# Mixture of experts behind convolution and attention: fixed first tiles, a one-hot gather for slot 0, and a reordered convolution end and last slot

## The chip, the cores and the metric

The kernel runs on one core of a Trainium2 chip. The metric is the device time of one execution in microseconds (us); the version before has a median of 236.17 us over three runs (235.69 to 236.37).

## The reference

The input x has shape (8, 192, 16, 16): 8 images, 192 channels, 256 pixels. Three parts follow each other, all in float32:

```python
x = x + conv(group_norm(x))          # 1x1 convolution over 192 channels and 28 local correlations ("taps")
t = tokens(x)                        # (8, 256, 192)
t = t + attention(layer_norm(t))     # causal, one head, d = 192
n = layer_norm(t)
e = argmax(n @ Wg.T + bg)            # top-1 of 8 experts; its softmax over one value is 1
t = t + (silu(n @ W1[e].T) * (n @ W2[e].T)) @ W3[e].T     # inner width 469
```

## The kernel before, in words

All matrix products with rounded operands are made as sums of a high and a low part (names ending in H and L), so that each product of the reference is several matmuls. The kernel is written engine by engine in program order, with semaphores between the engines; nothing is reordered by a planner.

**Convolution.** A loop over i = 0 to 11 (LAG = 4) handles image i in its norm, and image i - 4 in its convolution. On TensorE, iteration i does near_gram (L1125), group_sums at i = 2 (L1063), near_norms (L1082), and from i = 4 on conv (L1103), turn_taps (L1093) and conv_taps (L1118). keep_busy (L1248) issues matmuls whose result nobody reads. On ScalarE copy_taps (L515) copies the transposed taps, take_u and norm_image(0) (L585, the input of attention for image 0) stand at i = 10, copy_taps behind them. In the same iterations VectorE computes statistics (token_stats, L757) and leftover(0) (L812), one quarter of the low parts of expert 0's weights; GpSimd computes token_factors (L396, whose last instruction is L408) and weights_lo (L410).

**Attention.** step(t), t = 1 to 9, on every engine: scores, softmax, values, residual of image t - 1, statistics of image t - 2. Beside it the weights of the experts are loaded into two stage buffers by SyncE (L292), split into high parts by ScalarE (L522) and low parts by GpSimd (L410) and VectorE (L812). Expert 6's and 7's low parts are made by VectorE alone, in six pieces each (low_weights, L787).

**Routing.** gate (L818) finds a token's expert; counts (L1193) and positions (L838) give each token its row in a table in HBM, `xs`: every expert has a region, and `run` holds the running count. The last images are gates 4 (image 6) and 5 (image 7), both in step 9. scatter_tokens (L438) writes a tile of 128 tokens with an indirect DMA on GpSimd's queue. Behind the last gate VectorE computes from `run` which of 23 slots belongs to which expert and where it starts (L981 to L1010, `slot_expert`, `slot_row`), then the six pieces of expert 6 (L1012). Slots are in the order of the experts.

**Slots.** SyncE waits for all scatters and the table, then loads slot j's 128 rows (load_slot, L338), at most two at a time. ffn_step(j) on TensorE (L1325), ScalarE (L643) and VectorE (L1026) has three parts: `back` (transpose of gh(j - 1), L1343; its high part HH, L646, and low part HL, L1029; the products with W3, L1367 and L1368), `mid` (ten matmuls, L1076 to L1080, silu L649, product L1034) and `nxt` (transpose of the normalised rows of slot j + 1, L1358, parts FH L652 and FL L1037). norm_slot (L1017) normalises a loaded slot. Two adds (L1047, L1049) give the output rows, which GpSimd sends with an indirect DMA (L478). In steps 0 to 5 VectorE also makes one piece of expert 7's low parts. fill(40) (L1321) stands on TensorE ahead of the slots.

The lines that the sums touch most:

```python
            SCATTERS = {4: (0,), 5: (1,), 6: (2,), 7: (3, 4), 8: (5,), 9: (6,)}
            scatter_tokens(IMAGES - 1)
            norm_slot(0, 0, 1)
            for j in range(-1, SLOTS + 1):
                ffn_step(j, j % 2, j > 0, 0 <= j < SLOTS, j < SLOTS - 1, j // 2 + 2 if j + 2 < SLOTS else None)
                if 0 <= j < 6:
                    low_weights(EXPERTS - 1, (j,))
```

## Time and profile before

| | |
|---|---|
| median of the runs (range) | 236.17 us (235.69 to 236.37) |
| profiled execution, its own time | 237.56 us |
| its span, first to last instruction | 235.7 us |
| busy: TensorE, VectorE, ScalarE, GpSimd | 212.4, 170.6, 113.9, 105.0 us |
| mean granted TensorE clock | 0.96 of full speed |
| first expert product, end of the last TensorE matmul | 136.64, 229.69 us |

The times in all rows are microseconds from the start of the span. PE is TensorE's matmuls, PEld its weight loads, DVE is VectorE, ACT ScalarE, POOL GpSimd, SP SyncE; L1076 is line 1076 of the kernel. In a timeline row stand start, length, engine, line, operation, what it writes and reads, how many were merged, and in brackets the idle time before it with what ended it.

### The profile page before, as it was taken

What the parts mean: (1) busy time and instruction counts of PE and PEld (TensorE: products, weight loads), DVE (VectorE), ACT (ScalarE), POOL (GpSimd) and SP (SyncE); (2) the same over time, 40 slices, a digit from 0 to 9 for tenths busy, and PEclk for the clock granted to TensorE, in tenths of its full rate; (3) what the DMA queues carried; (4) which work ended last, traced back from release to release, by engine and by line L of the source; (5) the groups of instructions that cost most, each with busy time, mean ns of one, the idle gap of its engine ahead of it and who ended that gap; (6) DMA issues with size and microseconds to landing.
All of it is one profiled execution on the core that took longest, in us unless ns stands there. A gap on an engine that the chain in (4) does not pass through costs nothing.

```text
span 235.7 us, 4722 instructions
## 1 busy us (share of the span) xinstructions
PE 212.4 (90%) x1336; PEld 187.4 (79%) x1336; DVE 170.6 (72%) x554; ACT 113.9 (48%) x244; POOL 105.0 (45%) x131
## 2 busy tenths in 40 slices
PE   6977999987999979998889979999999999999970
PEld 3667889976999968987667768999999999999960
DVE  3696897774379859699787857888686767686741
ACT  2475655363199978897540033333334343434310
POOL 3266663829009997996766001131313131313131
PEclk9996899997699999999999999999999999999995
DMA  6991277856600562656211122233210000010100
GB/s 240 392 341 49 72 185 192 208 158 248 233 0 0 201 229 84 241 218 228 110 54 53 51 56 73 79 88 79 69 38 2 33 8 21 17 36 2 35 12 0
DMA packets 16343, 26.13 MB, mean 111 GB/s; under 512 B 3863, under 2 KB 12755, under 8 KB 15424
## 3 DMA queue, kind: packets, MB, share of 16 engines
q1 hardware_dynamic: 14448, 22.66, 30.3%
q0 software_dynamic: 1872, 3.18, 4.0%
q8 instruction: 12, 0.20, 0.3%
q14 instruction: 11, 0.09, 0.1%
HBM read 19.76 MB, written 6.76 MB: 113 GB/s over the span
## 4 chain that ended last, share of the span: by engine, by line
PE 55%; DVE 17%; POOL 7%; issue 7%; ACT 6%; DMA 4%; POOLq 1%; SPq 0%; DVEq 0%; ACTq 0%
PE bank L1367 8%; PE bank L1343 4%; PE bank L1076 4%; PE bank L1078 4%; PE bank L1080 4%; PE bank L1079 4%; PE bank L1077 4%; PE bank L1368 4%; PE bank L1251 3%; DMA stage<-in_w_all 2%; PE bank L1122 2%; PE bank L1358 2%; POOL ln L405 1%; DVE rows L881 1%; POOL wall L418 1%
## 5 line engine op out<-in xcount | busy, mean ns | idle before, releaser
L478 POOL DMA_INDIRECT out_rows<-yo,rows x23 | 22.4, 972 | 79.9 <-DVE yo L1049 70.0
L1367 PE MATMUL bank<-wall,HH 128*128 x92 | 29.4, 375 | 1.5 <-DVE HL L1029 1.5
L1034 DVE TENSOR_TENSOR gh<-gh,bank 128x470 f32<-128x470 f32 x23 | 14.8, 645 | 18.8 <-PE bank L1080 18.8
L646 ACT ACTIVATE HH<-bank 128x512 fp32r<-128x512 f32 x23 | 13.8, 599 | 27.9 <-PE bank L1343 27.9
L1208 PE MATMUL bank<-mH 128*128 128x512 f32 x98 | 24.4, 394 | 0.0
L652 ACT ACTIVATE FH<-bank 128x256 fp32r<-128x256 f32 x23 | 8.8, 385 | 30.7 <-PE bank L1358 30.7
L1368 PE MATMUL bank<-wall,HL 128*128 x92 | 23.1, 252 | 0.0
L1076 PE MATMUL bank<-wall,FH 128*128 x46 | 19.3, 419 | 1.2 <-DVE FL L1037 1.2
L1208 PEld LDWEIGHTS bank<-mH 128*128 128x128 f32 x98 | 17.8, 188 | 3.2
L444 POOL DMA_INDIRECT token_rows<-rows,posi x16 | 17.0, 1065 | 6.7 <-issue 4.4
L649 ACT ACTIVATE gh<-bank 128x470 f32<-128x470 f32 x23 | 13.0, 564 | 12.5 <-PE bank L1080 12.5
L1367 PEld LDWEIGHTS bank<-wall,HH 128*128 128x128 f32 x92 | 17.3, 188 | 1.8 <-issue 1.7
L1029 DVE TENSOR_TENSOR HL<-bank,HH 128x512 fp32r<-128x512 f32 x23 | 15.9, 691 | 3.3 <-ACT HH L646 3.1
L1368 PEld LDWEIGHTS bank<-wall,HL 128*128 128x128 f32 x92 | 17.6, 192 | 0.0
L1080 PE MATMUL bank<-wall,FL 128*128 x46 | 17.3, 376 | 0.0
L1078 PE MATMUL bank<-wall,FL 128*128 x46 | 17.3, 376 | 0.0
L1079 PE MATMUL bank<-wall,FH 128*128 x46 | 17.3, 375 | 0.0
L1077 PE MATMUL bank<-wall,FH 128*128 x46 | 17.2, 374 | 0.0
L1343 PE MATMUL bank<-small_sb,gh 128*128 128x128 f32 x92 | 13.9, 273 | 0.7 <-DVE gh L1034 0.6
L415 POOL TENSOR_TENSOR wall<-stage,wall 128x940 fp32r<-128x940 f32 x6 | 13.5, 2258 | 1.5 <-ACT wall L529 1.5
L418 POOL TENSOR_TENSOR wall<-stage,wall 128x768 fp32r<-128x768 f32 x6 | 12.8, 2134 | 0.0
L495 ACT ACTIVATE f32t<-xcm,gnb,grs 128x256 f32<-128x256 f32 x16 | 8.7, 593 | 7.6 <-POOL gnb L373 7.6
(228 smaller groups left out, 645.1 us busy)
## 6 DMA issues: line engine op xcount, KB each, us to landing
stage<-in_w_all SPq DMA_DIRECT2D x7, 1324.0 KB, 5.7
rows<-token_rows SPq DMA_DIRECT2D x23, 98.0 KB, 2.0
near_rows<-gram SPq DMA_DIRECT2D x8, 243.0 KB, 3.1
xcm<-in_x_cm SPq DMA_DIRECT2D x2, 768.0 KB, 7.0
rows<-in_x_tm SPq DMA_DIRECT2D x1, 1536.0 KB, 12.7
stage<-in_w_all SPq DMA_DIRECT2D x4, 331.0 KB, 4.0
token_rows<-emptyt SPq DMA_DIRECT2D x3, 294.0 KB, 4.6
taps_sb<-near_rows SPq DMA_DIRECT2D x8, 103.0 KB, 2.1
```

Of the source, the lines that this page charges most:

```text
L444: pool.indirect_dma_start(out=xs, out_offset=bass.IndirectOffsetOnAxis(ap=posi[:, j:j + 1].bitcast(U32), axis=0), in_=rows[:, j], in_offse ...
L478: pool.indirect_dma_start(out=out, out_offset=bass.IndirectOffsetOnAxis(ap=rows[:, j, C + 2:C + 3].bitcast(U32), axis=0), in_=yo[:, par], ...
L1029: nc.vector.tensor_tensor(HL[:, 1 - par].rearrange("p k x -> p (k x)"), bank[5][:], HH[:, 1 - par].rearrange("p k x -> p (k x)").bitcast(F ...
L1076: nc.tensor.matmul(dst, xh_a, y_a, start=True, stop=False)
L1077: nc.tensor.matmul(dst, xh_a, yl_a, start=False, stop=False)
L1078: nc.tensor.matmul(dst, xl_a, y_a, start=False, stop=False)
L1079: nc.tensor.matmul(dst, xh_b, y_q, start=False, stop=False)
L1080: return nc.tensor.matmul(dst, xl_b, y_q, start=False, stop=not more)
L1208: nc.tensor.matmul(bank[6][:], mH[:, 0:P], mH[:], start=True, stop=True)
L1343: mm = nc.tensor.transpose(bank[5][:, P * k:P * (k + 1)], gh[:, 1 - par, P * k:P * (k + 1)], ident)
L1367: nc.tensor.matmul(dst[:, 0:2 * C], HH[:, 1 - par, k], w(0, P, c0, c0 + 2 * C), start=(k == 0), stop=False)
L1368: mm = nc.tensor.matmul(dst[:, 0:C], HL[:, 1 - par, k], w(0, P, c0, c0 + C), start=False, stop=(k == FT - 1))
```

## The change

1. Front, TensorE: keep_busy(2) twice at i = 2, ahead of group_sums(2) and behind near_norms(0).
2. End of the convolution: ScalarE's copy_taps(6) goes ahead of norm_image(0); VectorE waits for ln1_ready ahead of leftover(0); GpSimd waits for leftover(0) ahead of weights_lo(0).
3. The first eight slots are the first tiles of the eight experts, at fixed rows of `xs` and with fixed weights on TensorE. The table is only for the other 15 slots. Slot 0 is loaded as soon as images 0 to 5 are scattered. The tokens of images 6 and 7 that belong to slot 0 are not scattered (their row gets NOWHERE added); VectorE builds one-hot tables (find_first), TensorE multiplies the rows of these images by them (gather), and VectorE adds the product to slot 0's rows (complete_first).
4. fill(40) goes; fill(2), fill(5) and, in step 0, fill(8) come. norm_slot(1) moves behind slot 0's `mid`. The table's arithmetic is cut into three functions, before and behind norm_slot(0) and behind step -1. Pieces of experts 6 and 7 are made in pairs in steps 0 to 5.
5. Last slot: the products on HH are made by themselves as soon as HH is there, all into 192 columns, then those on HL; one VectorE add instead of two.

```diff
+EMPTY = EXPERTS * REGION + PAD
+NO_TOKEN = 4096
+MORE = SLOTS - EXPERTS
+LATE = IMAGES - 2
+NOWHERE = 1 << 20
-WARM = 40
...
+        in_first = [a[:, 0:2 * P].rearrange("p (h q) -> p h q", h=HALVES) for a in (sc_sb, Pr)]
+        first_row = bank[3][:, 0:ROW]
...
-            sp.wait_ge(scattered, 16 * TILES)
+            def load_first_tile(e):
+
+                at = REGION * e + PAD
+                sp.dma_start(rows[:, e], xs[at:at + P]).then_inc(slot_in[e % 2], 16)
...
+            sp.wait_ge(scattered, 16 * HALVES * LATE)
             sp.wait_ge(empty_out, 16 * HEAD_PARTS)
+            load_first_tile(0)
+            sp.wait_ge(gathered, 1)
+            sp.wait_ge(scattered_late, 16 * (TILES - HALVES * LATE))
+            for e in range(1, EXPERTS):
+                if e >= 2:
+                    sp.wait_ge(slot_in[e % 2], 16 * (e // 2))
+                load_first_tile(e)
             sp.wait_ge(table_ready, 1)
...
             token_factors(1)
+            pool.wait_ge(wall_q, 1)
             weights_lo(0)
...
                     take_u(0, 0)
+                if i >= LAG:
+                    copy_taps(i - LAG)
+                if i == IMAGES + 2:
                     sc.wait_ge(ln1_ready, 2)
                     norm_image(0)
-                if i >= LAG:
-                    copy_taps(i - LAG)
...
+                    link(nc.vector.tensor_scalar(rsum[:], at, float(PAD + P), float(NOWHERE), ALU.is_lt, ALU.mult))
+                    nc.vector.tensor_tensor(posi[:, HALVES * a:HALVES * z], at, rsum[:], ALU.add).then_inc(pos_ready, 1)
+
+            def find_first(b):
...
+                nc.vector.tensor_tensor(in_first[b - LATE], row, at, ALU.is_equal).then_inc(in_first_ready, 1)
...
-                    for g in (4, 5):
-                        gate(g, link)
-                        positions(g, link)
+                    gate(4, link)
+                    positions(4, link)
+                    gate(5, link)
+                    find_first(LATE)
+                    positions(5, link)
+                    find_first(LATE + 1)
...
                     low_u(0, 0)
+                    ve.wait_ge(ln1_ready, 2)
                     leftover(0)
...
+            def complete_first():
+
+                ve.wait_ge(gathered, 1)
+                ve.wait_ge(slot_in[0], 16)
+                nc.vector.tensor_tensor(rows[:, 0, 0:C + 2], rows[:, 0, 0:C + 2], first_row[:, 0:C + 2], ALU.add)
+                token = rows[:, 0, C + 2:C + 3].bitcast(I32)
+                nc.vector.tensor_tensor(token, token, first_row[:, C + 3:C + 4], ALU.add).then_inc(first_whole, 1)
+                ve.wait_ge(first_whole, 1)
...
+            table_tiles()
             nc.vector.memset(gh[:, :, FE:FT * P], 0.0)
-            low_weights(EXPERTS - 2, range(6))
...
+                    if j == SLOTS:
+                        nc.vector.tensor_tensor(yo[:, 1 - par], y[:, 0:C], row, ALU.add).then_inc(y_taken, 1)
+                        return
...
+            complete_first()
             norm_slot(0, 0, 1)
+            table_ends()
             for j in range(-1, SLOTS + 1):
-                ffn_step(j, j % 2, j > 0, 0 <= j < SLOTS, j < SLOTS - 1, j // 2 + 2 if j + 2 < SLOTS else None)
-                if 0 <= j < 6:
-                    low_weights(EXPERTS - 1, (j,))
+                if j == -1:
+                    ffn_step(j, 1, False, False, True)
+                    table_slots()
+                elif j == 0:
+                    ffn_step(j, 0, False, True, False)
+                    norm_slot(1, 1, 1)
+                    ffn_step(j, 0, False, False, True, 2)
+                else:
+                    ffn_step(j, j % 2, True, j < SLOTS, j < SLOTS - 1, j // 2 + 2 if j + 2 < SLOTS else None)
+                if 0 <= j < 3:
+                    low_weights(EXPERTS - 2, (2 * j, 2 * j + 1))
+                elif 3 <= j < 6:
+                    low_weights(EXPERTS - 1, (2 * j - 6, 2 * j - 5))
...
                     counts(5)
+                    gather(LATE)
+                    fill(2)
+                    gather(LATE + 1)
+                    fill(5)
+
+            def gather(b):
+
+                pe.wait_ge(in_first_ready, b - LATE + 1)
+                for h in range(HALVES):
+                    mm = nc.tensor.matmul(first_row, in_first[b - LATE][:, h], rows[:, HALVES * b + h, :], start=(b == LATE and h == 0), stop=(b == IMAGES - 1 and h == 1))
...
                 if i == 2:
+                    keep_busy(2, c1("gm"))
                     group_sums(2)
                 if 2 <= i < LAG:
                     near_norms(i - 2)
+                if i == 2:
+                    keep_busy(2, c1("gm"))
...
-            fill(WARM)
...
+                if j == 0:
+                    fill(8)
                 if nxt:
...
+                    if j == SLOTS:
+                        for k in range(FT):
+                            for s in range(2):
+                                c0 = 3 * W12 + C * (2 * k + s)
+                                nc.tensor.matmul(dst[:, 0:C], HH[:, 1 - par, k], w(0, P, c0, c0 + C), start=(k + s == 0), stop=False)
+                        pe.wait_ge(hl_ready, j + AHEAD)
```

## Rows read from the trace of the kernel before

**Rows 1.** Windows: busy us (and instructions) of each engine, granted clock, DMA share, GB/s.
```profile
core 0: us, PE busy (x) PEld busy (x) DVE busy (x) ACT busy (x) POOL busy (x), PEclk, DMA share, GB/s
16.40:20.35 3.95, 1.41 (x11) 1.23 (x11) 3.54 (x15) 1.42 (x5) 1.73 (x3) 0.83 0.34 120
18.99:25.81 6.82, 5.48 (x19) 4.28 (x18) 4.93 (x21) 5.49 (x12) 5.36 (x10) 0.50 0.23 72
...
56.54:63.37 6.83, 6.83 (x31) 6.67 (x31) 1.33 (x5) 1.40 (x5) 2.36 (x2) 0.50 0.69 259
...
134.90:138.30 3.40, 2.17 (x11) 1.70 (x11) 1.02 (x4) 0.68 (x2) 0.00 (x0) 1.00 0.25 65
140.00:225.00 85.00, 84.96 (x518) 78.21 (x518) 64.67 (x155) 33.66 (x65) 20.05 (x21) 1.00 0.15 42
```

**Rows 2.** Chain that ended last, in order of time: start, us, what.
```profile
26.08 0.11 PE bank L1137
...
78.14 5.42 DMA stage<-in_w_all
...
112.38 0.35 PE bank L1235 x2
```

**Rows 3.** Timeline of the front, TensorE and VectorE.
```profile
23.05 2.76 PE L1251 MATMUL bank<-small_sb 128*128 128x384 f32 x4
...
23.76 0.74 DVE L745 SCALAR_TENSOR_TENSOR gram<-bank,rn,rnb 128x192 f32<-128x192 f32 x2
```

**Rows 4.** Timeline of the convolution's end: TensorE, ScalarE, GpSimd.
```profile
53.93 0.39 PE L1100 MATMUL bank<-small_sb,taps_sb 128*104 128x128 f32 x2
...
56.47 1.61 PE L1122 MATMUL bank<-wtap,taps_t 104*128 104x192 f32 x4 [1.62 <-ACT taps_t L520]
...
55.16 0.98 ACT L593 ACTIVATE xn<-rows,ln 128x192 f32<-128x192 f32 x2 [2.09 <-POOL ln L408]
...
62.55 0.38 ACT L520 ACTIVATE taps_t<-bank 104x256 f32<-104x256 f32 x1 [5.43 <-PE bank L1100]
...
45.38 0.19 POOL L408 TENSOR_TENSOR ln<-ln 128x2 f32<-128x2 f32 x1
...
53.85 1.17 POOL L408 TENSOR_TENSOR ln<-ln 128x4 f32<-128x4 f32 x1
```

**Rows 5.** Chain that ended last, the transfers of the handover.
```profile
128.92 2.51 DMA token_rows<-rows,posi
...
132.41 1.95 DMA rows<-token_rows
```

**Rows 6.** Timeline of the handover from attention to the slots, all engines.
```profile
124.95 1.07 POOL L444 DMA_INDIRECT token_rows<-rows,posi  x1 [1.25 <-DVE posi L851]
...
126.66 0.16 DVE L851 CAST posi<-bank 128x2 int32<-128x2 f32 x1
...
128.84 0.34 DVE L1002 TENSOR_TENSOR started<-small_sb,ends 128x184 f32<-128x184 f32 x1
...
126.65 8.32 PE L1208 MATMUL bank<-mH 128*128 128x512 f32 x36
...
134.39 0.38 DVE L1023 TENSOR_SCALAR xf<-rows 128x192 f32<-128x192 f32 x1 [0.35 <-DMA rows<-token_rows]
...
136.64 0.48 PE L1076 MATMUL bank<-wall,FH 128*128 x1 [1.16 <-DVE FL L1037]
...
140.28 0.47 PE L1076 MATMUL bank<-wall,FH 128*128 x1
```

**Rows 7.** Timeline of VectorE in the slots, with a piece of expert 7.
```profile
149.02 0.55 DVE L803 TENSOR_TENSOR wall<-stage,wall 128x384 fp32r<-128x384 f32 x1
149.49 0.68 DVE L1029 TENSOR_TENSOR HL<-bank,HH 128x512 fp32r<-128x512 f32 x1
150.79 0.65 DVE L1034 TENSOR_TENSOR gh<-gh,bank 128x470 f32<-128x470 f32 x1 [0.61 <-PE bank L1080]
```

**Rows 8.** Timeline of the last slot.
```profile
228.31 0.44 PE L1367 MATMUL bank<-wall,HH 128*128 x1 [1.50 <-DVE HL L1029]
...
229.72 0.36 DVE L1047 TENSOR_TENSOR yo<-bank,rows 128x192 f32<-128x192 f32 x1 [1.56 <-PE bank L1368]
```

More of the change, by code:

```diff
@@ L107 @@
 _at = 0
[L108 removed]
+for _n, _w in (("id", P), ("mask", 3 * P), ("wg", 2 * EXPERTS), ("bg", 2 * EXPERTS), ("desc", 2 * EXPERTS), ("base", EXPERTS), ("slot", MORE + 1), ("tri", 2 * P)):
     S2[_n] = (_at, _at + _w)
@@ L206, in build @@
         oh = sb("oh", [P, 2 * HALVES, EXPERTS], BF16, middle)
+        late_pos = (nmx, ssum)
         middle.close()
@@ L986, in _ @@
-            for n, d in enumerate((1, 2, 4)):
-                a, z = n % 2, 1 - n % 2
-                nc.vector.tensor_copy(ends[:, z, 0:d], ends[:, a, 0:d])
-                link(nc.vector.tensor_tensor(ends[:, z, d:EXPERTS], ends[:, a, d:EXPERTS], ends[:, a, 0:EXPERTS - d], ALU.add))
             starts = ends[:, 0]
-            link(nc.vector.tensor_tensor(starts, ends[:, 1], tiles_f[:], ALU.subtract))
-            wide = [P, SLOTS, EXPERTS]
-            slot = c2("slot")[:, 0:SLOTS]
-            slot3 = slot.rearrange("p (j a) -> p j a", a=1).to_broadcast(wide)
+            wide = [P, MORE, EXPERTS]
@@ L996, in over_slots @@
+            slot = c2("slot")[:, 0:MORE]
             def over_slots(v):
                 return v.rearrange("p (a e) -> p a e", a=1).to_broadcast(wide)
-            nc.vector.tensor_scalar(per_slot[:, 2], slot, ends[:, 1, EXPERTS - 1:EXPERTS], float(EMPTY), ALU.is_ge, ALU.mult)
-            nc.vector.scalar_tensor_tensor(out=tiles_f[:], in0=starts, scalar=float(P), in1=run[:], op0=ALU.mult, op1=ALU.add)
-            link(nc.vector.tensor_tensor(started[:], slot3, over_slots(starts), ALU.is_ge))
@@ L1010, in _, with table_tiles @@
-            nc.vector.tensor_tensor(slot_row[:], per_slot[:, 1], per_slot[:, 2], ALU.max).then_inc(table_ready, 1)
+            def table_tiles():
+                ve.wait_ge(pos_ready, len(gates) + AHEAD)
+                link(nc.vector.scalar_tensor_tensor(out=tiles_i[:], in0=run[:], scalar=float(P - 1), in1=c2("base"), op0=ALU.add, op1=ALU.subtract))
+                link(nc.vector.tensor_scalar(tiles_i[:], tiles_i[:], P.bit_length() - 1, None, ALU.logical_shift_right))
+                nc.vector.tensor_scalar(tiles_f[:], tiles_i[:], -1.0, 0.0, ALU.add, ALU.max)
+                link(nc.vector.tensor_scalar(ends[:, 0], tiles_i[:], -1.0, 0.0, ALU.add, ALU.max))
```

100 lines of the change are left out of this document (62 added, 38 removed).

## The prediction

> **What bounds the kernel now.** I read four views in this order: the stretches with the granted TensorE clock, the chain that ended last, the timeline around each edited place, and the page's totals. From 140 to 225 us TensorE is busy for 84.96 of 85 us at a clock of 1.00 [rows 1]: the expert slots are bound by TensorE, one slot per 3.9 us, and the change leaves their number at 23. What can be won lies before, between and behind those slots. The clock is at half (1.2 instead of 2.4 GHz) in two stretches of 6.8 us, 18.99 to 25.81 and 56.54 to 63.37; before the first, TensorE was busy for only 1.41 of 3.95 us, before the second it stood for 1.62 us, waiting for ScalarE's copy of the taps [rows 1, 4]. In the attention steps (64 to 119 us) the chain passes through ScalarE, VectorE, GpSimd and a stage load of 5.42 us [rows 2]; the change edits none of it, and each link starts from the one before. So whatever comes earlier at the end of the convolution comes earlier at the first slot, if no transfer has its own clock: the only one, expert 2's stage load, is issued at about 59 us, lands by 65 and is read at 75. Between attention and slots stands the handover: GpSimd's last scatter, 2.51 us to its landing, the load of slot 0, 1.95 us [rows 5], then 2.25 us from the normalisation at 134.39 to the first expert product at 136.64 [rows 6].
>
> **The front: two times keep_busy(2) at i = 2.** A keep_busy(2) is 4 instructions; those at 23.05 took 2.76 us at half clock [rows 3], so about 1.3 us at full. The first goes in front of group_sums(2), the second behind near_norms(0). Both fall into the stretch 16.40 to 20.35, in which 2.5 us were idle [rows 1]: they cost nothing while the full clock lasts. If it lasts, near_gram(2) and the old keep_busy run at full speed, but the gain is small: near_gram(3), next behind that keep_busy on TensorE (it began at about 25.0), also waits for VectorE's gram copy of 23.76, lasting 0.74 us [rows 3], so it can begin at 24.5 at best, and the next links hang on VectorE and GpSimd. I take 0.35 us. Bounds: 1.0 gained, or 1.3 lost if the clock falls all the same (the second batch then takes 2.6 us and is late by 1.3).
>
> **The end of the convolution.** The taps of image 6 leave TensorE at 54.32 (start 53.93, 0.39) [rows 4], but ScalarE copied them behind norm_image(0), which began at 55.16 after a wait for GpSimd's L408; TensorE stood from 54.85 to 56.47. Now the copy comes first: ready at 54.7, conv_taps(6) at 54.8. L408 took 1.17 us with VectorE's leftover(0) beside it, and 0.19 us for the earlier gang without it [rows 4]. The new wait in front of leftover(0) takes that away, so ln1_ready comes at 54.1, and norm_image(0) runs right behind the copy, 54.65 to 55.65 (0.98). The Trainium skill, GPSIMD Engine Reference, section Specifications, says that GpSimd's SBUF interfaces are shared with VectorE and contended by VectorE instructions with two SBUF inputs; leftover is one, and the trace agrees (1.17 against 0.19). Were the delay something else and to stay, xn would come at 56.15 and 0.5 us less would be won. TensorE has no gap over 0.2 us left there, so I expect the clock to stay full. From 55.75: turn_image, scores, half a conv and turn_taps are 21 instructions at about 0.11 [rows 2] plus first-instruction and end costs, 2.65 us; taps copy at 58.4 instead of 62.55, hence 4.15 less. Queued behind the new waits are leftover(0) (until 55.3) and GpSimd's weights_lo(0) (0.4 later, until 59.3, so the stage load of expert 2 lands at about 65.5, read at 71 in the new time): hidden. I take 4.0. Bounds: 1.6 (the clock still falls: only conv_taps(6) moved, 56.47 to 54.8) and 4.6.
>
> **The handover**, told in the times of before. posi of image 7 is ready at 126.82 [rows 6]. Added in front of it on VectorE: two small instructions (one per late image, 0.2 each as neighbours of 0.16 are spaced) and the one-hot table of image 6, 256 elements. A table of 184 elements took 0.34 [rows 6]; I take 0.42, of which 0.3 falls into the wait for the counts. posi: 127.3; second table: 127.75. TensorE then makes two plain f32 products, 0.35 us each (two instructions each) [rows 2], done with their end at 128.75; the table arithmetic on VectorE lies beside them. Two adds (0.36 and 0.17): 129.4. Slot 0's own load waits only for images up to 5, whose scatters landed before 125, so it is there. norm_slot(0) therefore starts at 129.45 instead of 134.39: 4.95 earlier. table_ends (about 1.0 us of small instructions) now lies between it and FL, beside the transpose and ScalarE's copy: 0.1 late. First expert product: 131.8, that is 4.85 earlier. The removed fill(40) cost nothing (8.32 us for 36 instructions of this kind, all over before the load) [rows 6]; its successors fill(2) and fill(5) end before 130.1.
> The second slot starts 3.64 us after the first now (136.64 to 140.28). In the change norm_slot(1) runs behind slot 0's gate product, and TensorE does fill(8) (8 by 0.23 = 1.85) before the transpose. Products 2.15, fill 1.85, transpose to product 1.6 as in 135.05 to 136.64: 5.6. It gives back 1.96, so **2.9** stays. Slot 1's load: SyncE has queued it, with loads 2 to 7, behind slot 0's load, the products (over at 128.75) and the last scatter, which starts at 129.5 (posi plus 0.85 as at 124.95, plus one scatter), lands at 132.0; load issued by 132.5, there at 134.5; norm_slot(1) can start at 134.9. Slack 0.4. GpSimd's queue gets nothing else. Bounds of the handover: 4.1 (the fill hides more than I think) and 1.9 (load 1 late by 1 us).
>
> **VectorE within the slots.** Expert 6's low parts leave the front (there hidden by the load) and go in pairs into steps 0 to 2, expert 7's in pairs into steps 3 to 5 instead of singly into 0 to 5. One piece spaces its neighbour by 0.47 us (149.02 to 149.49), and VectorE idled 0.61 before gh [rows 7]. A second piece uses that idle up, and HL (0.68) ends 0.1 to 0.3 after TensorE wants it. Once shifted, the excess per step is near nothing for the pieces of W1, W3 and about 0.2 for the others. Together 0.4 lost; bounds 0 and 1.5 (0.3 in each of five steps). Table_slots in step -1 takes 1.7 us while TensorE computes slot 0 for 2.15: hidden; without that cover gh(0) is late by as much.
>
> **The last slot.** TensorE waited for HL (0.68) at 228.31 [rows 7, 8]; the eight products on HH now start that much earlier, and with 12 instructions at 0.11 instead of four pairs at 0.29 the last ends 0.55 earlier. The second VectorE add (0.40 spacing, 229.72 to 230.12) goes. Gain 0.95; bounds 0.7 and 1.1.
>
> **Sum:** 0.35 + 4.0 + 2.9 - 0.4 + 0.95 = **7.8 us**. The profiled execution took 237.56 us (span 235.7 and 1.9 around it): 229.8. The median of the runs shown, 236.17, lies 1.4 lower, so I forecast 228.4. Image 6's and 7's other additions (iotas at the start) lie beside the first loads.
>
> **Rivals.**
> (1) The clock falls in the handover. There are now gaps of 0.55, 0.3, 1.2 and 0.6 us between 127.4 and 137.4, where the fill was solid. For: after 1.62 us standing it fell. Against: 134.90 to 138.30, with 2.17 of 3.40 busy, kept 1.00 [rows 1]. Price: half of a 6.8 us stretch, 3.4: 231.8. Chance 0.17.
> (2) It falls in the convolution's end all the same: gain there 1.6, 230.8. For: a shorter wait for ScalarE stands ahead of it, at 49 to 51 us, and adds to what is left; against: the clock kept 1.00 through that one. Chance 0.10.
> (3) The front's filling does not hold the clock: -1.3 instead of +0.35, 230.0. Chance 0.08.
> (4) The one-hot tables, two SBUF inputs each, block GpSimd's scatters as leftover blocked L408: up to 0.4 each, load 1 up to 0.8 later than said, slack gone, 228.9. This is the rule of the Trainium skill named above. Chance 0.05.
> (5) Slower than before: the low clock started by rival 1 is not given back, since VectorE's pair steps open new gaps in each slot. Each us at half clock costs 0.5, so it decides from 15.6 us at half clock; over steps 0 to 6 (27 us) it would be 13.5 lost, 241.9 in the end. Against: both low stretches ended after 6.8 us [rows 1], under broken work too. Chance 0.04.
> The change does what it says if the first eight loads are issued without the table; I see no way in which it wouldn't.
>
> **Chances.** My forecast has 0.56, with 227.3 to 229.6 as its own range. The overall range reaches to 231.4, taking in rivals 2 to 4 and the lower half of 1, and down to 227.1. About 0.3% (0.7 us) is what a measurement of this kernel can tell from no change. Faster 0.96, same 0.01, slower 0.03 (rival 5, a quarter of it mild).
>
> **What would show it.** Right: clock 1.00 from 16 to 26 and through the convolution's end; the tapsT copies of images 6 and 7 no more than 4.1 us apart (now 6.5); posi of image 7 to norm_slot(0) in 2.6 us (now 7.7); first to second slot 5.6 us; slots at 3.9; a last wait of TensorE of about 0.8. Wrong: a 0.50 in any stretch; a wait of VectorE for slot 1's load; over 4.2 us per slot in steps 1 to 5. The sum fails if the steps' pace were set by a stage load and not by what came before.

## The result, and the profile after

The changed kernel took 233.56 us (median of 4 runs, 233.16 to 233.58), the kernel before beside it 236.27 (235.69 to 237.3): ratio 0.9874, 95% interval 0.9824 to 0.9924. It is faster, by 2.7 us and not by the 7.8 forecast, and it lies above the range. The profiled execution took 233.54 us, with a span of 231.7; against the profiled execution of before (237.56, span 235.7) that is 4.0 less. (The ratios are worked out from the undisturbed executions of both kernels, so one can differ from the quotient of its two medians.)

From the page of the changed kernel:

```profile
span 231.7 us, 4547 instructions
PE 209.1 (90%) x1331; PEld 182.4 (79%) x1331; DVE 171.4 (74%) x559; ACT 113.9 (49%) x244; POOL 105.3 (45%) x133
PEclk9999999999999999999999999999999999999995
```

TensorE's clock (PEclk, in tenths) is 9 or more in every slice up to the last. The stretches that answer to [rows 1], of the changed kernel (columns as there):

```profile
16.40:20.35 3.95, 3.95 (x27) 3.17 (x26) 3.75 (x13) 2.03 (x4) 2.07 (x4) 1.00 0.50 180
18.99:25.81 6.82, 5.97 (x31) 3.91 (x30) 5.01 (x23) 5.11 (x12) 4.11 (x7) 1.00 0.12 42
55.33:60.06 4.73, 4.73 (x40) 4.37 (x38) 2.47 (x6) 2.24 (x7) 3.48 (x4) 1.00 0.89 302
140.00:225.00 85.00, 83.05 (x509) 76.06 (x507) 64.66 (x153) 32.01 (x62) 22.27 (x22) 1.00 0.14 40
```

Both stretches at half clock are gone, as forecast: 18.99 to 25.81 has 1.00 now, and so has the convolution's end, whose 4.73 us TensorE fills without a gap. The last row reaches past the last product of the changed kernel, so its 1.95 idle us are mostly the end.

The timeline of the changed kernel at the places of [rows 4], [rows 6] and [rows 8]:

```profile
55.37 0.20 POOL L427 TENSOR_TENSOR ln<-ln 128x4 f32<-128x4 f32 x1
55.87 0.39 ACT L540 ACTIVATE taps_t<-bank 104x256 f32<-104x256 f32 x1 [1.28 <-PE bank L1170]
59.78 0.38 ACT L540 ACTIVATE taps_t<-bank 104x256 f32<-104x256 f32 x1 [1.96 <-PE bank L1170]
124.81 0.16 DVE L877 TENSOR_TENSOR posi<-ssum,rsum 128x2 int32<-128x2 f32 x1 [0.24 <-DVE rsum L876]
126.94 0.43 DVE L1078 TENSOR_SCALAR xf<-rows 128x192 f32<-128x192 f32 x1
129.18 0.45 PE L1146 MATMUL bank<-wall,FH 128*128 128x470 f32 x1 [1.09 <-DVE FL L1092]
131.38 2.02 PE L1278 MATMUL bank<-mH 128*128 128x512 f32 x8
134.55 0.48 PE L1146 MATMUL bank<-wall,FH 128*128 128x470 f32 x1 [0.50 <-DVE FL L1092]
222.49 1.22 PE L1459 MATMUL bank<-wall,HH 128*128 x8 [0.77 <-ACT HH L667]
222.86 0.97 POOL L498 DMA_INDIRECT out_rows<-yo,rows  x1 [2.52 <-DVE yo L1107]
224.20 0.36 DVE L1103 TENSOR_TENSOR yo<-bank,rows 128x192 f32<-128x192 f32 x1 [1.12 <-PE bank L1463]
227.24 0.97 POOL L498 DMA_INDIRECT out_rows<-yo,rows  x1 [3.41 <-DMA out_rows<-yo,rows]
```

The taps copies of images 6 and 7 stand 3.91 us apart (before 6.50), posi of image 7 and slot 0's normalisation 2.13 apart (before 7.7), first and second slot's products 5.37. All three were forecast. What was not forecast is the last row: the send of the last slot had its data at 224.56 and went out at 227.24, after a wait for a transfer. The kernel before had 0.80 us between the two.

Span against span, each step as the two traces show it (us won; a copy of XH ends each image's work, and the last copy of HH opens the last slot's second half):

| stretch | forecast | two profiles | before, after |
|---|---|---|---|
| start to XH(0) | +0.35 | -1.52 | 48.81, 50.33 |
| XH(0) to XH(1), the convolution's end | +4.0 | +4.29 | 14.02, 9.73 |
| XH(1) to the second slot's first product | +2.9 | +2.96 | 77.45, 74.49 |
| from there to the last copy of HH | -0.4 | -0.64 | 86.56, 87.20 |
| that copy to the last output row | +0.95 | +0.82 | 3.63, 2.81 |
| last output row to the end of the span | 0 | -1.91 | 5.23, 7.14 |
| sum | 7.8 | 4.00 | 235.7, 231.7 |

Four of six terms came out within 0.3 us in this pair of profiles. The first missed by 1.9 and the last by 1.9, and the medians, 1.3 us closer together than the profiled executions, hold a third miss. The experiments look for these three.

### The profile page after: what moved, and what is told of

Read it like the earlier page. It is cut to its first block, busy times and chain, and to the rows that moved or that the text cites. A ratio compares the mean times of both kernels' runs of the same rounds, so it can differ in the third digit from the quotient of the medians.

```text
span 231.7 us, 4547 instructions
## 1 busy us (share of the span) xinstructions
PE 209.1 (90%) x1331; PEld 182.4 (79%) x1331; DVE 171.4 (74%) x559; ACT 113.9 (49%) x244; POOL 105.3 (45%) x133
## 4 chain that ended last, share of the span: by engine, by line
PE 59%; DVE 16%; POOL 6%; issue 6%; DMA 6%; ACT 5%; POOLq 1%; DVEq 0%; ACTq 0%
PE bank L1468 8%; PE bank L1146 4%; PE bank L1333 4%; PE bank L1150 4%; PE bank L1149 4%; PE bank L1148 4%; PE bank L1147 4%; PE bank L1429 4%; PE bank L1469 3%; DMA stage<-in_w_all 2%; PE bank L1446 2%; PE bank L1192 2%; DMA taps_sb<-near_rows 2%; DMA out_rows<-yo,rows 1%; PE bank L1141 1%
## 5 line engine op out<-in xcount | busy, mean ns | idle before, releaser
L498 POOL DMA_INDIRECT out_rows<-yo,rows x23 | 23.2, 1011 | 76.9 <-DVE yo L1107 61.5
L1468 PE MATMUL bank<-wall,HH 128*128 (+1 forms) x88 | 28.1, 374 | 0.3 <-issue 0.3
L1469 PE MATMUL bank<-wall,HL 128*128 (+1 forms) x88 | 22.1, 251 | 0.0
L1146 PE MATMUL bank<-wall,FH 128*128 (+1 forms) x46 | 19.3, 419 | 1.6 <-DVE FL L1092 1.6
L1278 PE MATMUL bank<-mH 128*128 128x512 f32 x73 | 19.3, 400 | 0.0
L1150 PE MATMUL bank<-wall,FL 128*128 (+1 forms) x46 | 17.3, 376 | 0.0
L1149 PE MATMUL bank<-wall,FH 128*128 (+1 forms) x46 | 17.2, 375 | 0.0
L1148 PE MATMUL bank<-wall,FL 128*128 (+1 forms) x46 | 17.2, 375 | 0.0
L1147 PE MATMUL bank<-wall,FH 128*128 (+1 forms) x46 | 17.2, 374 | 0.0
L1468 PEld LDWEIGHTS bank<-wall,HH 128*128 128x128 f32 x88 | 16.5, 188 | 0.8 <-issue 0.8
L1469 PEld LDWEIGHTS bank<-wall,HL 128*128 128x128 f32 x88 | 16.8, 191 | 0.0
L1278 PEld LDWEIGHTS bank<-mH 128*128 128x128 f32 x73 | 13.1, 188 | 2.1
```

The lines of the kernel that those rows point to most:

```text
L498: pool.indirect_dma_start(out=out, out_offset=bass.IndirectOffsetOnAxis(ap=rows[:, j, C + 2:C + 3].bitcast(U32), axis=0), in_=yo[:, par], ...
L1146: nc.tensor.matmul(dst, xh_a, y_a, start=True, stop=False)
L1147: nc.tensor.matmul(dst, xh_a, yl_a, start=False, stop=False)
L1148: nc.tensor.matmul(dst, xl_a, y_a, start=False, stop=False)
L1149: nc.tensor.matmul(dst, xh_b, y_q, start=False, stop=False)
L1150: return nc.tensor.matmul(dst, xl_b, y_q, start=False, stop=not more)
```

## The experiments

### Which parts of the change pay: front, convolution's end, last slot

**front_undone.** The changed kernel without the two pairs.

```diff
-                if i == 2:
-                    keep_busy(2, c1("gm"))
                     group_sums(2)
...
-                if i == 2:
-                    keep_busy(2, c1("gm"))
```

> The changed kernel without the two pairs of filling products at image 2. Theory (filling neutral to useful): the 1.5 us that the front lost by 49 us began with TensorE at the half clock up to 11 us, before any filling that changed, so it stays; without the pairs the clock falls at about 19 as in the kernel before, and the time is 0 to 1.0 longer: 233.6 to 234.6, the forecast's term being 0.35. Rival (filling costs): the pairs stand ahead of the group sums and the image's products and cause the loss: the time falls by 0.6 to 1.5, to 232.1 to 233.0, the clock in 19 to 26 us being lower all the same.

232.82 us (4 runs, 232.6 to 235.7; ratio 0.9829, 0.9739 to 0.9919; the medians of before were 236.5 to 237.9 in the five comparisons told here). XH(0) came at 50.60 instead of 50.33. The same stretch as above, of this kernel:

```profile
18.99:25.81 6.82, 5.27 (x24) 4.59 (x25) 5.02 (x23) 4.14 (x10) 4.05 (x7) 0.67 0.14 43
```

The pairs hold the clock up to 25.8 us: it is 1.00 over this stretch in all 15 profiles with them and fell to half at 18.9 to 21.3 us, for 6.8 us, in all five without. What that is worth at XH(0) is small and not settled. The seven profiles with the pairs and the same late start (told below) have it at 50.21 to 50.59, mean 50.38, this one without them at 50.60; so a gain of 0.35 fits, and so does nearly none. And in four profiles with the pairs (fewer_fill, pool_later, combined, start_held) the clock fell a little later instead, at 27.2 to 28.7 us for 3.4 us; of fewer_fill:

```profile
25.81:33.00 7.19, 6.92 (x45) 6.74 (x45) 5.51 (x19) 2.88 (x7) 3.55 (x5) 0.76 0.47 131
```

The first pixels were late here too (10.14 us), so the 1.5 us do not come from the pairs. This run's time is 0.7 below the changed kernel's all the same; why is seen further down.

**front_only.** The kernel before with the two pairs alone.

> The kernel before, with only the two pairs of filling products at image 2. Theory (neutral to useful): 235.3 to 236.3, the forecast's term being 0.35 gained; TensorE's clock stays 1.00 from 16 to 26 us. Rival (the pairs cost the 0.6 to 1.5 us that the front of the changed kernel lost): 236.9 to 237.8. What TensorE's clock does before 11 us has to be as in one of the two kernels in either case, since the pairs stand behind it.

237.52 us beside 237.1 of before, ratio 0.9991 (0.995 to 1.0031): no change that shows. The fourth norm copy came 0.36 us earlier (31.04 against 31.40) and the seventh 0.30 (44.81 against 45.11), but the eighth 0.22 later (48.75 against 48.53), and so XH(0) at 49.03; what held the eighth was not followed up. First pixels at 9.36, as in the kernel before.

**conv_end_only.** The kernel before with the new order at the convolution's end alone.

```diff
             token_factors(1)
+            pool.wait_ge(wall_q, 1)
             weights_lo(0)
...
                     take_u(0, 0)
+                if i >= LAG:
+                    copy_taps(i - LAG)
+                if i == IMAGES + 2:
                     sc.wait_ge(ln1_ready, 2)
                     norm_image(0)
-                if i >= LAG:
-                    copy_taps(i - LAG)
...
                     low_u(0, 0)
+                    ve.wait_ge(ln1_ready, 2)
                     leftover(0)
```

> The kernel before, with only the order at the convolution's end changed: ScalarE copies the taps before it normalizes image 0, VectorE waits for the norms before the left-over weights, GpSimd's first low weights wait for the quarter pieces. Theory (the steps are paced by what came before them): all of the 4.3 us that the two traces show there comes out at the end: 236.27 - 4.0 = 232.3, between 231.8 and 232.8. Rival (a stage load or another engine paces the attention steps and takes part of it back): 233.0 to 235.5.

234.74 us, ratio 0.988 (0.9811 to 0.9949): 2.4 less than before by the medians (237.1 in this call), where the profiled execution (233.78, span 231.9) has 3.8 less than the profiled one of before. The time lies in the rival's range, but in its profile the gain of the stretch did reach the slots: from XH(1) to the first expert product are 74.05 us (before 73.81). XH(0) to XH(1) took 9.74 us.

**conv_end_undone.** The changed kernel with the old order there (the same diff, reversed).

> The changed kernel with the old order at the convolution's end (ScalarE normalizes image 0 before it copies the taps, no wait of VectorE or GpSimd for the norms and quarter pieces): the handover, the front and the last slot alone. Theory (the parts add up): 4.3 us later from image 0 to image 1 (13.9 to 14.1 instead of 9.7 us), and all but 0.1 to 0.5 of it at the end: 237.1 to 237.8, if the last send is delayed as in the changed kernel. Rival (stage loads or the earlier handover absorb a part): 235.0 to 236.9.

237.03 us in 10 runs, 234.0 to 238.55; 3.45 above changed_again of the same call. XH(0) to XH(1) took 12.83 and not 13.9 to 14.1. So in both tests what the order gives in the end is 2.4 to 3.5, and the stretch itself is not the same each time. The old order was profiled five times; here are three of them, TensorE from XH(0) + 5.0 to XH(1), columns as in [rows 1]. Kernel before:

```profile
53.81:62.83 9.02, 7.40 (x38) 7.07 (x37) 2.47 (x6) 2.24 (x8) 5.09 (x4) 0.65 0.76 270
```

front_only:

```profile
54.03:61.90 7.87, 6.25 (x40) 5.92 (x38) 2.47 (x6) 2.23 (x7) 5.10 (x4) 0.78 0.75 248
```

before_again (told below), the kernel before unchanged:

```profile
54.02:60.25 6.23, 4.61 (x40) 4.42 (x38) 2.47 (x6) 2.24 (x7) 5.12 (x4) 1.00 0.76 250
```

The first and the third are the same program. After the same wait of 1.62 us the granted clock is 0.65, 0.78 or 1.00 over the stretch, and the stretch 9.02, 7.87 or 6.23 us; the other two (before_pool_more and conv_end_undone) have 0.78 as well. The wait is not the only thing that counts: before_again kept the clock, and alone of the five it lacks a wait of 0.3 to 0.5 us for the previous taps copy ahead of it (it has one of 0.43 for a transfer in that place). Whether that decides is not shown. The five spans from XH(0) to XH(1) are 14.02, 12.87, 12.84, 12.83 and 11.23, mean 12.76. The new order took 9.72 to 9.74 in all of its 15 profiled executions, at a clock of 1.00. It is worth 1.5 us where the clock had not fallen, 4.3 where it fell longest, 3.0 on the mean of the five. The execution profiled before the prediction was the slowest of them there, and the only one at half clock for 6.8 us; three were so for 3.4.

conv_end_undone also tests the row that the prediction tied to the Trainium skill. GpSimd's last instruction of the norms, in conv_end_undone:

```profile
55.43 1.17 POOL L427 TENSOR_TENSOR ln<-ln 128x4 f32<-128x4 f32 x1
```

With VectorE's leftover(0) beside it 1.17 us, behind the new wait 0.20 (the changed kernel's row above); so in all five profiles of the old order (1.16 to 1.17) and in all 15 of the new (0.20). The Trainium skill, GPSIMD Engine Reference, Specifications, has GpSimd's SBUF interfaces contended by VectorE instructions with two SBUF inputs; undoing the wait brings the 1 us back, so the trace agrees here.

**last_slot_undone.** The changed kernel with the old order of the last slot.

```diff
-                    if j == SLOTS:
-                        nc.vector.tensor_tensor(yo[:, 1 - par], y[:, 0:C], row, ALU.add).then_inc(y_taken, 1)
-                        return
...
-                    pe.wait_ge(hh_ready, j + AHEAD)
-                    if j < SLOTS:
-                        pe.wait_ge(hl_ready, j + AHEAD)
+                    pe.wait_ge(hl_ready, j + AHEAD)
...
-                    if j == SLOTS:
-                        for k in range(FT):
...
-                        return w_mid
```

> The changed kernel with the last slot in its old order: TensorE waits for both halves of the last hidden layer, forms the full products, VectorE adds twice. Theory (the forecast's term): last output row ready 0.8 to 1.0 later against the last copy of the hidden layer (from 2.81 to about 3.63 us, as in the kernel before), and, where the send before has landed by then, the time 0.8 to 1.0 longer; where it has not, the time is unchanged, since the last send waited for that landing until 227.24 anyway. Rival (the reordering gives nothing): 2.8 us from the last copy to the last row.

The last row came 3.62 us after the copy instead of 2.81: the term of 0.8 is real. But the time was 231.68 us (231.31 to 232.34, ratio 0.9757, 0.9685 to 0.983): undoing a gain made the kernel faster. Its last send went out 0.80 us after its row, not 2.68.

### The late last send

**send_first.** The changed kernel; the send is issued ahead of the wait for the one before it. The buffer that this wait frees is not written until later, so nothing else moves.

```diff
             def send_slot(j, par):
...
-                if j:
-                    pool.wait_ge(out_sent[1 - par], 16 * ((j + 1) // 2))
-                    pool.sem_inc(yo_free, 1)
                 pool.wait_ge(y_taken, j + 1 + AHEAD)
...
                 pool.indirect_dma_start(...).then_inc(out_sent[par], 16)
+                if j:
+                    pool.wait_ge(out_sent[1 - par], 16 * ((j + 1) // 2))
+                    pool.sem_inc(yo_free, 1)
```

> The changed kernel, in which each slot's output is sent before GpSimd waits for the landing of the send before it, not after. Theory (late send): at the end of the changed kernel the last send was issued at 227.24 although its rows stood ready about 1.9 us earlier, because the send before it (222.86) had not landed; without that wait the last send goes out at about 225.4 and the median is 231.7 (233.56 - 1.9). Rival (queue in order): the last send would land behind the one before it anyway, so that issuing it early gives nothing or at most 1 us: 232.6 to 233.6.

232.67 us (231.02 to 234.74, ratio 0.9737, 0.9649 to 0.9824). The last send went out 0.80 us after its row, and the span ended 5.47 us after the row (7.15 in the changed kernel, 5.26 in the kernel before). So 1.7 of the 1.9 come back: the last send landed 2.1 us after its issue though the one before it was still on its way, so no queue holds it up, only the wait.

But why is the send before it late in the changed kernel and not in last_slot_undone, whose send stands in the same place? The DMA queues say it. The stretch from 223 to 227 us of the changed kernel (queue and kind: packets, MB, share; then issues with the median from issue to landing):

```profile
DMA packets 49, 0.02 MB, mean 4 GB/s; under 512 B 48, under 2 KB 48, under 8 KB 48
q8 instruction: 1, 0.02, 1.4%
q0 software_dynamic: 48, 0.00, 0.8%
out_rows<-yo,rows POOLq DMA_INDIRECT x1, 3.4
```

and of fewer_fill (below), from 222 to 226:

```profile
DMA packets 48, 0.00 MB, mean 0 GB/s; under 512 B 48, under 2 KB 48, under 8 KB 48
q0 software_dynamic: 48, 0.00, 0.7%
out_rows<-yo,rows POOLq DMA_INDIRECT x2, 2.1
```

One packet of instructions, 16 KB (queue 8 moves 0.20 MB in 12 packets over the run), lies beside the 48 small packets of the send in the first, none in the second. The send lands 3.4 us after its issue with it, 2.1 without. That is not this send's alone. Over the 20 profiles, of the sends of slots 6 to 22, the 237 without an instruction packet in their time landed after 2.1 to 2.4 us, and the 47 behind whose issue one of queue 8 began 0.9 to 2.2 us later took 3.1 to 4.3; a packet that began ahead of the issue cost nothing that shows, where none followed it. In the slots queue 8's packets lie 15 to 20 us apart; in the changed kernel the twelfth and last falls at 224 us, in last_slot_undone (8 TensorE instructions fewer) and front_undone (16 fewer) there is no twelfth. The Trainium skill has pieces that fit: engines' instruction memory is refilled in 16 KiB blocks (Runtime: NRT & Kernel Launch, Terms), and a DMA engine drains a whole packet before it turns to another queue (DMA: Bandwidth & Descriptors, Queues, rings and completion order). The packet's size agrees; which DMA engine the two shared no row here shows.

**fewer_fill.** To move that packet, six products and their six weight loads are left out in the attention steps, over 100 us ahead of it:

```diff
                 if 2 <= t < IMAGES:
-                    fill(5)
+                    fill(4)
```

**changed_again.** The changed kernel itself, on the chip of the three that follow.

> The changed kernel without any edit, on the chip of the next three. Theory (its losses are systematic): group sums 1.7 us and first pixels at 10.1 as in its first profile, a 16 KB instruction transfer at 224 or 225 us, between the last two sends, the last send issued 2.4 us or more after the last row stands ready (0.8 where nothing delays it), and the time 233.2 to 234. Rival (both were chance): one of the two is absent here, and the time is 231 to 232.5.

> The changed kernel with four filling products instead of five in each of the attention steps 2 to 7: 12 TensorE instructions fewer (6 products, 6 weight loads), nothing else. The trace of the changed kernel shows 12 instruction transfers of 16 KB on queue 8, the last at 224 us; front_undone (16 instructions fewer) and last_slot_undone (8 fewer) show 11, none after 211 us. Theory (that transfer runs beside the last send but one and makes it land 4.3 instead of 2 to 3 us after its issue, and the last send waits for it): 11 transfers, the last send 0.8 to 1.4 us after the last row, and the time 1.3 to 1.9 below changed_again's. Rival (the late landing belongs to the new order of the last slot): the last send is as late as in the changed kernel, and the time is the same within 0.5.

changed_again: 233.58 us, ratio 0.9821 (0.976 to 0.9881), packet at 224 us, last send 2.66 us after its row, first pixels at 10.12: all as in the first profile. Against this call's 237.85 of before it is 4.3 us faster; the gain depends on how the kernel before fares. fewer_fill: 231.9 us, ratio 0.975 (0.9688 to 0.9813), 11 packets, the last at 208, and the last send 1.38 us after its row. The packet theory holds for 1.3 of the 1.9, for which its rival (the new last slot itself) falls. (From issue to landing the late send took 3.4 us, not the 4.3 of the expectation.) The other 0.5 is the rival's: with its row 0.82 earlier, the send meets the landing of the one before even at 2.1 us. Over all profiles, from last row to last send: 2.66 to 3.19 with the packet beside it (five), 1.35 to 1.38 without (three), 0.80 with the send ahead of its wait (six), 0.80 to 0.91 with the old last slot and no such packet (six). Of the 1.7 us between the two medians not all is the packet's: fewer_fill's profiled execution also had the earlier start.

### The late start

In the changed kernel ScalarE's first pixels began at 10.13 instead of 9.24 us. TensorE's timeline in the changed kernel:

```profile
2.29 4.21 PE L1333 MATMUL bank<-taps_sb 128*128 128x384 f32 x6 [2.29 <-POOL taps_sb L375]
6.29 1.72 PE L1141 MATMUL bank<-mq,small_sb 128*128 128x8 f32 x8
```

and in fewer_fill, whose code is the same up to 60 us:

```profile
2.29 4.21 PE L1333 MATMUL bank<-taps_sb 128*128 128x384 f32 x6 [2.29 <-POOL taps_sb L375]
6.29 1.31 PE L1141 MATMUL bank<-mq,small_sb 128*128 128x8 f32 x8
7.45 3.47 PE L1333 MATMUL bank<-small_sb 128*128 128x384 f32 x10
```

The group sums take 1.03 us in the kernel before, 1.72 here; the filling behind them takes 3.47 us for ten at full clock (2.4 GHz), while in the changed kernel its products stand 0.64 us apart, the half clock's (1.2 GHz) spacing, up to 10.6 us, and 0.32 from 11.1 on. (The clock's own column has 1.00 there and can't be used; durations tell.) So the clock rose at about 10.9 us, where it rose before 6.1 in the kernel before. Nothing of TensorE's changes up to there; only GpSimd has two instructions more.

**pool_later.** The changed kernel with `iota(place_row)` and the `tensor_scalar` of the late rows behind token_factors(2).

> The changed kernel with its two extra GpSimd instructions of the start (the row of places, the late images' tags; 2.52 to 3.08 us) moved behind the convolution. In the three profiles of kernels with them the first group sums took 1.71 to 1.73 us and ScalarE's first pixels began at 10.11 to 10.14; in the three without, 1.03 us and 9.24 to 9.36. Theory (these instructions are what shifts the start): group sums 1.03 us from about 6.1, first pixels at 9.24 to 9.4, and the time 0.9 to 1.5 shorter. Rival (something else of the changed program does it: its loads, its instruction streams, its place in memory): first pixels at 10.1 again and the same time as the changed kernel.

First pixels at 9.56, XH(0) at 49.45: 0.9 us earlier. Yet 233.63 us (ratio 0.9827, 0.975 to 0.9904): the attention steps, XH(1) to XH(7), took 46.29 us against 43.43, and the packet lay beside the send again (3.02). The 2.9 us come from four places: XH(3) to XH(4) took 0.6 longer (ScalarE waited 2.03 us for a stage load up to 80.95, 1.80 in the changed kernel), XH(4) to XH(5) 1.4 longer, XH(5) to XH(6) 0.4 less, and the last step 1.25 longer (a wait of 1.10 for a stage load up to 104.59). From XH(4) to XH(5) the clock was at half:

```profile
85.21:88.62 3.41, 3.41 (x16) 3.41 (x17) 3.17 (x15) 2.19 (x6) 1.69 (x3) 0.50 0.16 65
```

It fell there in three profiles of 20 (send_first and front_only are the others), with 8.09 us for that step instead of 6.70, and these are the three with the longest wait for the stage load, 2.03 to 2.19 us; the others have at most 1.85. That the longer wait makes the clock fall is likely and not tested.

**before_pool_more.** The kernel before with two such instructions added at the start.

> The kernel before with the same two GpSimd instructions added at the same place, their results unused. Theory (they shift the start): group sums 1.7 us, first pixels at 10.1. Rival: group sums 1.03 us, first pixels at 9.2 to 9.4.

237.26 us (one run). Group sums 1.07 us, first pixels at 9.48, nearer the rival: the instructions alone don't do it.

**fill_earlier.** send_first, with the memset of the taps first and four products. (Two other waits on the same semaphore are raised to match the new order.)

```diff
+            nc.gpsimd.memset(taps[:]...).then_inc(filled, 1)
             nc.gpsimd.memset(half_c[:], -0.5).then_inc(filled, 1)
...
-            nc.gpsimd.memset(taps[:]...).then_inc(filled, 1)
...
-            pe.wait_ge(filled, 4)
-            keep_busy(3, taps[:]...)
+            pe.wait_ge(filled, 1)
+            keep_busy(4, taps[:]...)
```

> The changed kernel with the send moved ahead of its wait, as in send_first, and with GpSimd's memset of the taps first, so that TensorE's filling starts at about 1.3 instead of 2.29 us; four filling products instead of three. Theory (TensorE's clock rises after it has been kept busy, and the start decides whether by 6 us or only by 11): the clock is up before the first group sums, they take 1.03 us, the first pixels begin at 9.3 or earlier, and the time is 0.9 to 1.5 below send_first's. Rival (the rise comes at a set place of the run, whatever TensorE did): half clock to 11 us again, first pixels at 10.1 or later, since one more product at 1.28 us is in the way.

232.35 us (ratio 0.9802, 0.9724 to 0.988). TensorE began at 1.84, not 1.3; the clock was up for the second filling (3.47 us), but the fourth product pushed the group sums to 7.09 and the pixels to 10.58. XH(0) came at 50.13, 0.2 earlier than in the late starts. The times lie with send_first's; the forecast saving of 0.9 to 1.5 did not come.

**before_again, fewer_fill_again, pool_later_again.** Three programs a second time, a profile each.

> The kernel before without an edit. Theory (the program sets when the clock rises): group sums 1.03 us from 6.1, first pixels at 9.24 to 9.4. Rival (chance): at least one of the three repeats of this call differs from its first profile by over 0.3 us at the first pixels.

> fewer_fill without a further edit. Theory (program): group sums 1.3 us, first pixels at 9.7 again. Rival (chance; six of the seven kernels with these GpSimd instructions in place and TensorE starting at 2.29 rose at 11.2): group sums 1.7 us, first pixels at 10.1.

> pool_later without a further edit. Theory (program): group sums 1.16 us, first pixels at 9.56 again. Rival (chance): another value between 9.2 and 10.1. For the steps: 43.4 to 44.5 us from image 1 to image 7 if the 46.3 of its first profile was scatter of the stage loads, 46 again if the moved instructions cause it.

235.23, 232.31 and 232.78 us. First pixels at 9.17 (9.24), 10.12 (9.71) and 9.37 (9.56). In fewer_fill the clock rose by 7.5 us once and not until 11 the other time, with the same program: chance has a part. But it isn't even chance. With those GpSimd instructions in place and TensorE's three products from 2.29 us, the changed kernel and its offspring had the late start in 8 of 9 profiles, with them moved in 0 of 3, and the kernel before and its offspring in 0 of 5, before_pool_more among them. What tips it stays open. before_again's 235.23 is 2.3 below the profiled execution from which the forecast started. pool_later_again's steps took 44.06 us, so the 46.29 was scatter.

**start_held, start_held_again.** two_edits (below) with `keep_busy(4, ...)` for `keep_busy(3, ...)` at 2.29 us, so that long products last until the clock rises.

> two_edits with four filling products instead of three at TensorE's start. Theory (the rise comes between 5.6 and 7.6 us where TensorE is kept in long products until then, and is missed where the short group sums follow at 6.1): the second filling after the group sums at full clock (3.47 us for 10 products instead of 4.8 to 5.2), group sums of image 1 at 11.3 to 11.6 instead of 12.7, image 0's rows at 49.6 to 49.9 instead of 50.3, the time 0.3 to 0.7 below two_edits' 231.6: 230.9 to 231.3. Rival (chance): half clock to 11.2 us again, and the time 0.6 to 1.2 above two_edits', since the fourth product costs 1.28 us there.

> The same kernel as start_held, a second look. Theory: as there. Rival (chance): it differs from start_held by over 0.3 us at the first pixels, or is late in both.

Early in both: second filling 3.47 us, its group sums at 12.03 and 11.47 instead of 12.65. But the first pixels came at 10.96 and 10.24, for the fourth product has to be waited for, and the times are 231.75 (230.83 to 232.22; ratio 0.9778, 0.9748 to 0.9808) and 231.19. The cure costs what it brings. With fill_earlier, four products gave three early rises in three.

### The versions that keep the gains

**combined.** send_first, fewer_fill and pool_later together.

> The changed kernel with three edits: the send ahead of its wait (send_first), fewer filling products (fewer_fill), GpSimd's two extra instructions of the start moved (pool_later). Theory (each removes its own loss): image 0 ready at about 49.4 instead of 50.3, last send 0.8 us after the last row, the time 2.3 to 2.8 below changed_again's, 230.7 to 231.3. Rival (the steps' stage loads take the front's gain back, as in pool_later, whose steps took 46.3 us from image 1 to image 7 against 43.4): only the end's 1.3 to 1.9 is left, 231.6 to 232.3.

Its profiled execution has the shortest span of all profiles (229.3), 231.18 us; but the median of six is 233.39 (231.18 to 234.6; ratio 0.9834, 0.9777 to 0.9892), above fewer_fill's 231.9 in the same call and 0.2 below changed_again's. That lies above the theory's range and the rival's. The five unprofiled executions left no trace, so where they lose is not known.

**two_edits.** fewer_fill and send_first only.

> The changed kernel with fewer_fill's edit and send_first's, and nothing moved on GpSimd. Theory (the moved instructions of combined do harm in unprofiled runs, the other two edits only gain): last send 0.8 us after the last row, 11 instruction transfers on queue 8, the time 230.8 to 231.9, at or below fewer_fill's 231.9. Rival (the difference of combined and fewer_fill was scatter of the stage loads): 231.9 to 233.4.

231.62 us (231.02 to 232.51), ratio 0.9771 (0.9723 to 0.9819): the theory's range. Its last send, although the start was late (10.24) here:

```profile
224.04 0.36 DVE L1103 TENSOR_TENSOR yo<-bank,rows 128x192 f32<-128x192 f32 x1 [1.12 <-PE bank L1463]
225.20 0.97 POOL L494 DMA_INDIRECT out_rows<-yo,rows  x1 [1.53 <-DMA out_rows<-yo,rows]
```

fewer_fill, measured beside changed_again, is 1.7 us faster by the medians (the intervals of the two ratios overlap between 0.976 and 0.9813); two_edits is level with fewer_fill (0.9771 and 0.975, each in its own call), and its last send no longer waits. A packet beside the last send but one still costs a little in this order: the span ended 5.47 (send_first) and 5.83 us (fill_earlier) after the last row, 5.26 in two_edits.

## Why the prediction was wrong, step by step

- **The convolution's end** came out as said, in mechanism (copy first, no gap, clock 1.00, GpSimd's 1.17 gone) and, against that trace, in size (4.29 for 4.0). What failed is the step that carried it over: "the median of the runs shown, 236.17, lies 1.4 lower, so I forecast 228.4" took the 1.4 off both kernels. Much of it sat in the very stretch that the change shortens: 14.02 us in that execution, 12.76 on the mean of five. On that mean the term is 3.0 and not 4.0.
- **The handover** was right: slot 0 normalised 4.68 us earlier against XH(1) (4.95 said), first product 4.69 (4.85), second slot after 5.37 (5.6), 2.96 won (2.9). Rival 1 did not come: clock 1.00, TensorE's longest wait there 1.09 us. conv_end_undone has it without the new convolution's end: from XH(1) to the normalisation 66.81 us (before 71.56). Rival 4 did not come either: GpSimd's last three scatters, around the tables, took 0.97 us each. One row was misread, without harm: the old fill was not "all over before the load" but ran to 134.97, with the load there by 134.4, just ahead of the transpose at 135.05.
- **The slots** lost 0.64 for 0.4, **the last slot** won 0.82 for 0.95 up to its row.
- **The front**: the pairs held the clock as said, and rival 3 did not come; their 0.35 is neither shown nor refuted. The 1.5 us were lost ahead of them. "Image 6's and 7's other additions (iotas at the start) lie beside the first loads" counted only what the instructions cover, and the sum took the start of that one trace as given. It is a draw, and the changed kernel draws worse: 0.9 us hang on when the clock first rises, and between 0.2 and 0.6 more on the loads (the pixel load landed in 7.0 us in the trace of before, in 8.2 to 9.2 in all others). On the means, XH(0) is 49.06 in the five profiles that start like the kernel before and 50.34 in the nine of the changed kernel and its offspring that keep its start: 1.3 lost.
- **The end** had no term, and that is the step that failed outright. The sum stopped at the last output row. A send waits for the one before it; in the kernel before the last two stood 3.32 us apart, the landing takes 2.1 and the next issue 0.94 more, so the slack was 0.28. The change brings the last row 0.82 earlier, of which 0.54 is lost on that slack (1.34 instead of 0.80 from row to send), and the packet takes 1.3 on top. The row that could have warned is the wait of a send for a transfer: before, three sends waited so, 9.9 us in sum.
- **The steps** moved with what came before them in the first pair (43.52 and 43.43 us), but scatter from 43.2 to 46.3 over the profiles. In the slowest, two stage loads came late and the clock was at half for 3.4 us, as told at pool_later. "If no transfer has its own clock" was too sure: an earlier front need not arrive, as pool_later and combined show. How often, 3 to 10 runs a kernel can't say.

By the measured terms: front -1.3, convolution 3.0 (both means of several profiles), handover 2.96, slots -0.64, last slot 0.82, end -1.91 (one pair), which is 2.9; measured were 2.7 (0.9824 to 0.9924, so 1.8 to 4.2) and 4.3. The prediction's "0.3%" for what can be told from no change was too small: the intervals here reach 0.3 to 0.9% to either side.

## What to carry to other kernels

A profile is one draw: a stretch that looks worth removing was perhaps long by chance, so compare the profiled time with the median and charge the surplus to the stretch that varies, not evenly. Follow each gain to the last transfer's landing, not to the last computed row; in a two-buffer send loop put the wait behind the send, since the freed buffer is needed later than the next send. And look for instruction packets in the DMA queues: a dozen instructions more or less, far from the place, can shift one onto a send that ends the kernel.

## What the runs showed of the hardware that was not expected

- One 16 KB instruction packet beside an indirect send of 48 small packets: landing 3.4 us instead of 2.1 (3.1 to 4.3 instead of 2.1 to 2.4 over all sends of slots 6 to 22); present in all five profiles with the last send over 2.6 us late, absent from the three at 1.3 to 1.4.
- The same program after the same 1.62 us wait of TensorE kept its clock once (1.00) and lost it another time (0.65 over 9.02 us). In the attention steps the clock fell in three profiles of 20, those with the longest wait for one stage load, and cost 1.4 us in that step, of which the next gave back 0.4.
- At the start the clock rose anywhere from under 6 to about 11.5 us (the products' spacing goes from 0.64 to 0.32 us). With `keep_busy(4)` it was up before the second filling in three profiles of three, with `keep_busy(3)` in 9 of 17; the same program could do either.
